# Causal attention with exact maxima: one order for maxima and exponentials, two rings of PSUM banks, and a diagonal masked in SBUF

## The reference

```
x = L0_attn_x
xn = _layernorm(x)
s = _L0_attn_ref(xn, ...)             # 16 heads of 8 features
g = _silu(_L0_ffn_ref(xn, ...))       # soft mixture of 8 experts
x = x + s * g
xn = _layernorm(x)
s = _L1_attn_ref(xn, ...)
g = _silu(_L1_ffn_ref(xn, ...))       # routed experts, a top 2 and a top half per expert
x = x + s * g

# attention, in both layers
q, k = _rope(q), _rope(k)
scores = jnp.einsum('bhqd,bhkd->bhqk', q, k) * D ** (-0.5)
scores = jnp.where(causal, scores, -jnp.inf)
weights = jax.nn.softmax(scores, axis=-1)
out = jnp.einsum('bhqk,bhkd->bhqd', weights, v)
```

## Time and profile before

| | us |
|---|---|
| three timed runs | 1244.29, 1248.29, 1241.22 (median 1244.29) |
| span of the profiled execution | 1235.5 |
| what lies around the span (median less span) | 8.8 |
| PE busy | 895.0 (72%) |
| DVE busy | 600.8 (49%) |
| ACT busy | 426.9 (35%) |
| POOL busy | 77.7 (6%) |
| attention, layer 0, first maxima to last output | about 208 to 611 |
| attention, layer 1 | about 816 to 1222 |

### The profile page before, as it was taken

One profiled execution on the slowest core, in us unless ns is written; L12 is line 12 of the kernel. 1 busy time (PEld: TensorE's weight loads), 2 busy tenths in 40 slices (PEclk: granted clock), 3 DMA queues, 4 the chain that ended last, 5 costly groups with the idle time before them and its releaser, 6 DMA issues.

```text
span 1235.5 us, 16046 instructions
## 1 busy us (share of the span) xinstructions
PE 895.0 (72%) x5604; PEld 448.6 (36%) x5604; DVE 600.8 (49%) x1338; ACT 426.9 (35%) x546; POOL 77.7 (6%) x51
## 2 busy tenths in 40 slices
PE   4377788797876967868865522947886968879786
PEld 3134576243333333433433222612333433333333
DVE  4573202663553734735172545495643725537442
ACT  1243332144424344435612400013434334344354
POOL 1710002000000000000007200000000000000000
PEclk9679998577978789889976755855978869689899
DMA  6110001001001010010022200000000010010001
GB/s 248 66 37 1 1 1 45 33 1 40 12 29 39 0 39 20 19 39 1 4 92 77 76 26 0 1 0 1 6 35 35 6 39 12 27 39 0 39 1 34
DMA packets 19563, 37.62 MB, mean 30 GB/s; under 512 B 2880, under 2 KB 12864, under 8 KB 19008
## 3 DMA queue, kind: packets, MB, share of 16 engines
q1 hardware_dynamic: 19264, 36.79, 8.2%
q10 hardware_dynamic: 256, 0.26, 0.1%
HBM read 29.44 MB, written 7.34 MB: 30 GB/s over the span
## 4 chain that ended last, share of the span: by engine, by line
PE 46%; DVE 16%; issue 16%; DMA 8%; POOL 5%; ACT 4%; SPq 4%; DVEq 0%; ACTq 0%; POOLq 0%
PE ps L939 42%; DVE maxes L882 8%; DMA R<-k_thirds 7%; SPq L435 3%; PE ps L1181 2%; SPq L437 2%; POOL rope L485 2%; POOL rope L488 1%; ACT R L633 1%; POOL third L492 1%; ACT R L628 1%; PE ps L1158 1%; DVE bnst L668 1%; ACT third L553 1%; ACT third L555 1%
## 5 line engine op out<-in xcount | busy, mean ns | idle before, releaser
L939 PE MATMUL ps<-R 128*128 128x128 f32 (+10 forms) x2240 | 568.5, 364 | 166.0 <-DMA R<-k_thirds 74.8
L882 DVE TENSOR_REDUCE maxes<-ps 128x1 f32<-128x512 f32 (+3 forms) x640 | 385.6, 635 | 321.9 <-PE ps L939 310.7
L628 ACT ACTIVATE R<-ps 128x1024 f32<-128x1024 f32 (+1 forms) x320 | 292.6, 937 | 409.8 <-PE ps L939 405.2
L939 PEld LDWEIGHTS ps<-R 74*128 74x128 bf16 (+4 forms) x2240 | 237.2, 133 | 468.6 <-issue 171.7
L939 PE MATMUL ps<-R,vgrp 128*32 128x512 f32 (+3 forms) x1536 | 176.9, 532 | 0.0
L939 PE MATMUL ps<-maskq,identb 128*128 128x128 bf16 x512 | 122.6, 257 | 0.0
L939 PE MATMUL ps<-maskk,identb 128*128 128x128 bf16 x512 | 121.8, 238 | 0.0
L939 PEld LDWEIGHTS ps<-maskk,identb 128*128 128x128 bf16 x512 | 55.0, 107 | 26.1 <-issue 16.4
L939 PEld LDWEIGHTS ps<-maskq,identb 128*128 128x128 bf16 x512 | 58.6, 114 | 5.2 <-issue 4.4
L939 PE MATMUL ps<-count,R 128*128 128x1 f32 x64 | 18.3, 357 | 54.7 <-DVE R L823 52.1
L510 POOL COPY vgrp<-vals 128x288 f32 (+1 forms) x16 | 7.1, 453 | 793.1 <-PE ps L939 793.0
(11 more groups left out here) (147 smaller groups left out, 539.0 us busy)
## 6 DMA issues: line engine op xcount, KB each, us to landing
R<-q_thirds SPq DMA_DIRECT2D x96, 96.0 KB
R<-k_thirds SPq DMA_DIRECT2D x96, 96.0 KB
R<-in_w SPq DMA_DIRECT2D x2, 2048.0 KB, 11.6
q_thirds<-third SPq DMA_DIRECT2D x8, 384.0 KB, 2.6
k_thirds<-third SPq DMA_DIRECT2D x8, 384.0 KB, 3.3
rot<-in_rot SPq DMA_DIRECT2D x1, 1024.0 KB, 5.2
R<-in_spread SPq DMA_DIRECT2D x1, 1024.0 KB, 5.7
out<-x SPq DMA_DIRECT2D x4, 256.0 KB, 2.3
```

The source lines that it names most:

```text
L628: act.activation(probs[SLOT[step]][:, h, 0:w], flat[:, 1024 * (n % 2):1024 * (n % 2) + w], ACT.Exp, scale=SCALE).then_inc(s.exp, 1)
L882: dve.tensor_reduce(dst, src, AX.X, ALU.max).then_inc(s.max_read, 1)
L939: return pe.matmul(out_, lhsT, rhs, start=first, stop=last)
```

## The change

Attention is written anew on all engines; both layers' groups are unrolled (no loop). The work of maxima, exponentials and value products stays the same in columns. In parts:

- **Maxima.** They have operands of their own, `qmx` and `kmx`, in the space of the `rope` buffers: four products (two thirds times two) of eight features, MR = 32 partitions for each head, so four heads fill the 128 partitions. A unit has two heads in a pair of banks: 1024 columns, 18 units for a group. Matmuls of the two heads alternate. Two PSUM pairs (banks 0 and 1, 2 and 3) form a ring. In the four units of diagonal blocks one matmul per bank writes the mask first and the scores are added.
- **Exponentials.** 36 units of 512 columns in a ring of three banks (4 to 6), which the shift transpose and the output transposes share. They carry no mask; GpSimd zeroes the masked triangle of `probs` with `affine_select`, ten instructions for a group. `probs` is a ring of 18 units.
- **Values.** Ten steps; queries of the first half, then of the second, both in bank 7, which ACT must have copied out between them (`pvout`).
- **Output.** ACT copies the transposed sums to `raw`; DVE divides once for each batch entry.
- **Order.** `attention_order` lays out all eight groups by estimated times.
- **Loads.** For each group 16 DMAs of 32 KB (`load_for_max`) and six of 192 KB (`load_for_exp`), each two groups ahead of their use. The two shift DMAs are issued by SyncE now, in the same list.

```diff
+UNITS, STEP = [], []
+for half in range(2):
...
+PATTERN = [[(i, 0, 512)] for i in (4, 5, 6, 7)] + [
+    [(2, 0, 256), (3, 0, 256)], [(6, 512, 256), (7, 512, 256)],
+    [(1, 0, 128), (3, 256, 128), (5, 512, 128), (7, 768, 128)],
+    [(i, P * i, 128) for i in range(4)], [(i, P * i, 128) for i in range(4, 8)]]
+NM = 2 * len(PATTERN)
...
+MAX_US, EXP_US, TOP_US, SHIFT_LAG_US, LEAD_US = 1.25, 0.56, 0.7, 3.0, 3.5
+PV_LAG, OUT_LAG = 5, 3
...
+            def load_for_max(L, g):
+                r = g % 2
+                for h in range(HG):
+                    head = slice(g * HG * D + h, (g + 1) * HG * D, HG)
+                    rows_h = slice(MR * h, MR * h + MR)
+                    for n in range(2):
+                        rows_n = slice(MR * h + 16 * n, MR * h + 16 * n + 16)
+                        sp.dma_start(qmx[rows_n, r, :],
+                                     q_dram[L][n:n + 1, head, :].to_broadcast([2, D, T])).then_inc(s_mload[r], 16)
+                        sp.dma_start(kmx[rows_n, r, :], k_dram[L][0:2, head, :]).then_inc(s_mload[r], 16)
+
+            def load_for_exp(L, g):
...
+                for i in range(3):
+                    rows_i = slice(3 * D * i, 3 * D * i + 3 * D)
+                    sp.dma_start(qop[rows_i, r, :, :].rearrange("p h t -> p (h t)"),
+                                 q_rows[i:i + 1].to_broadcast([3, D, HG * T])).then_inc(s_xload[r], 16)
+                    sp.dma_start(kop[rows_i, r, :, :].rearrange("p h t -> p (h t)"), k_rows).then_inc(s_xload[r], 16)
+
+            def attention(L):
+                cells = L * CELLS
+                for what, g, *arg in ORDER:
+                    n = L * NG + g
+                    if what == "shift":
+                        cells += 1
+                        sp.wait_ge(s_cells_read, cells)
+                        for part in range(2):
+                            sp.dma_start(qop[KR + part:KR + part + 1, g % 2, :, :],
+                                         shiftT[HG * TB * part:HG * TB * part + HG * TB, :]
+                                         ).then_inc(s_shift_in[g % 2], 16)
+                    elif what == "exp" or what == "out":
+                        cells += 1
+                        if arg[0] == NU - 1 and g + 2 < NG:
+                            sp.wait_ge(s_cells_full, cells)
+                            load_for_exp(L, g + 2)
+                    elif what == "max" and arg[0] == NM - 1 and g + 2 < NG:
+                        sp.wait_ge(s_rows_full, (n + 1) * NM)
+                        load_for_max(L, g + 2)
...
+                        if arg[0] == first + count - 1 and diagonal:
+                            slot = first % RING
+                            pool.wait_ge(s_cells_read, cells)
+                            for column in diagonal:
+                                where = probs[:, slot:slot + count, column:column + P]
+                                pool.affine_select(where, where, [[0, count], [1, P]], ALU.is_ge, 0.0, base=0,
+                                                   channel_multiplier=-1).then_inc(s_masked, 1)
...
+                    if what == "max":
...
+                        if arg[0] == 0:
+                            pe.wait_ge(s_mload[r], (L * NG // 2 + g // 2 + 1) * 16 * 16)
+                        if units >= 2:
+                            pe.wait_ge(s_rows_read, units - 1)
+                        pair = 2 * (units % 2)
+                        if diagonal:
+                            for k in range(2):
+                                mm(bank(pair + k).rearrange("p (n c) -> p n c", n=4), identb[:, :], maskq[:, :].unsqueeze(1).to_broadcast([P, 4, P]), True, False)
+                        c = 0
+                        for i, k0, w in pieces:
+                            for k, h in enumerate(heads):
+                                rows_h = slice(MR * h, MR * h + MR)
+                                last = mm(bank(pair + k)[:, c:c + w], qmx[rows_h, r, P * i:P * i + P],
+                                          kmx[rows_h, r, k0:k0 + w], not diagonal, not diagonal or c + w == BANK)
+                            c += w
+                        last.then_inc(s_rows_full, 1)
+                        units += 1
+                    elif what == "exp":
+                        if arg[0] == 0:
+                            pe.wait_ge(s_xload[r], (L * NG // 2 + g // 2 + 1) * 6 * 16)
+                            pe.wait_ge(s_shift_in[r], (L * NG // 2 + g // 2 + 1) * 2 * 16)
+                        if cells >= 3:
+                            pe.wait_ge(s_cells_read, cells - 2)
+                        for j, h, q, w, c in UNITS[arg[0]]:
+                            last = mm(bank(at)[:, c:c + w], kop[0:KM, r, h, P * j:P * j + P], qop[0:KM, r, h, q:q + w])
+                        last.then_inc(s_cells_full, 1)
+                        cells += 1
```

## The result

| | us |
|---|---|
| before, runs beside it | 1242.76 median of 4 (1239.36 to 1248.29) |
| after | 1371.63 median of 4 (1362.52 to 1373.17) |
| ratio | 1.104 (1.098 to 1.110) |
| profiled execution | span 1371.1, whole time 1373.17 |

The change makes the kernel 10% slower; 1296 was predicted, and 1371.6 lies above the range's end of 1360. The 8.8 us that the prediction put around the span are 2.1 in the execution that was profiled. In all that follows, an execution more than 1.5% above the fastest of its kernel is left out (one of e2's four, 1048.7 us, three of e4's four, 1298.4 to 1305.9, one of e7's four, 3585.6, and two of four each of e9 and e14, 1088.3 to 1110.6), and a kernel's time is the median of the rest.

A forecast was written before the change was run, and what follows sets the result against it. Bound: shift rows behind SyncE's 22 loads, steady groups 56.2 us. Changes 29.5 - 3.8 + 25.6 + 0.7 = 52 make the span 1287.5; with 8.8 around it 1296 us, range 1255 to 1335, with rivals 1180 to 1360.

The forecast's parts named there:

- the cold stretch: TensorE from a group's first exponential to its last maxima unit: 23.2 us warm, half clock adds 3.8, giving 27.0.
- its signs: In the profile: first exponentials wait 15 to 20 us for shift rows, clock 0.5 after; spacing 54 to 58 in groups 1 to 4.
- The shift behind the loads: SyncE's queue: shift rows land 29.2 us after the last maxima unit, from 11.8 issue, 16.5 data and 0.9.
- Rival (1): SyncE's queue: the shift waits for issue but not data, 9.8 us less at six boundaries per layer, 1178; chance 0.18.
- Rival (3): Loads for the maxima: the 32 KB loads crawl on one engine, 19.6 us, +73 in all, 1369; chance 0.09.
- TensorE's warm work: TensorE per group at full clock: pieces sum to 30.0 us (24.6 to 32.6), plus 1.2 of waits.
- rival (2): TensorE: strips overlap everywhere without switch cost, 4.0 us less over the 27.0, 1240, no change; chance 0.10.
- The sum: Attention per layer, from first group to last group and tail: 394.9 us together, against 365.4 and 369.3 before.
- GpSimd's mask: GpSimd zeroing masked exponentials: 3.5 to 9.4 us a group on an idle queue, hidden except in the tail.
- DVE's pitch: DVE's reductions for maxima: 1.17 us a unit, 18 units 21.1, with the final maxima 22, beside TensorE's 31.
- ACT's 22 us: ACT per group: 36 exponentials 20 us, with four small copies and the shift 22, beside TensorE's 31.
- Rival (4): Whole kernel: the plan works, no stall at first exponentials, groups of 31.2 us, time near 990; chance 0.02.

The follow-up runs named there:

- e2: Kernel after, with SyncE issuing the shift rows first and the loads of both kinds behind them: 1034.4 us, ratio 0.828.
- e4: Kernel after, with 90 unread mask matmuls (62 in the last but one group) while TensorE waits for the shift rows: 1271.0 us.
- e7: e2 plus unread mask matmuls behind the maxima units ahead of the first exponential and at the starts of groups 0 to 6: 1030.9 us, ratio 0.835.
- e9: e2 with the maxima's matmuls on 64 rows instead of 32, zeros in the other head's rows: 1077.2 us.
- e14: e2 with the maxima's matmuls on 64 rows, all data (sums over two heads, output not the reference's): 1079.6 us.
- e5: Kernel after, with the maxima's matmuls on all 128 rows (sums over four heads, output not the reference's): 1269.6 us, ratio 1.024.
- e0s: Not a run: the first exponential units of successive groups; the distance from one to the next is called a group.
- e0: Not a run: a group's first exponential unit, which waits for the shift rows.
- e3: Kernel after, with the six exponential loads moving an eighth of their columns from group 2 on (output not the reference's): 1216.5 us, ratio 0.977.
- e8: e7 plus 12 unread mask matmuls ahead of the last group's first exponential and one behind every third exponential there: 1024.3 us, ratio 0.826.
- e12: e2 with the maxima's matmuls on all 128 rows, zeros in the other heads' 96: 992.3 us, ratio 0.802.
- e6: Kernel after, with the two heads of a maxima unit one after the other instead of alternating: 1371.4 us, ratio 1.107.

## Why the prediction was wrong

**The step that failed** is the cold stretch: "half clock after a stall of 20 us adds 3.8 as in the earlier trace rows: 27.0". The runs show 10.6 instead (32.3 cold against 21.7 warm). Two things are in it. The 8.3 us of the earlier trace rows belong to a list without strips: e5, which takes the strips away, is at full clock again after 3.7 to 6.8 us and falls by 102 us, where the kernel after takes 18.8 to 34.1. And they were read from one group; five others of the same trace had shown 13.5 to 16.2 us and one 19.9, so even that list didn't support one short figure. The prediction took a time of recovery from one group of one mix of instructions and put it under another mix. Of its signs the wait came (20.3 us where 15 to 20 was said) and the spacing of e0s didn't (60.9 to 65.0 us where 54 to 58 was said). Why strips hold the clock down is open.

**The shift behind the loads: right, and nearly to the digit.** Unit 17 to e0 was to take 29.2 us; it takes 29.05 (517.86 to 546.91). Its parts were off in ways that cancel: loads come every 0.64 us and not 0.74 (16 take 10.4, not 11.8), and data and landing take the rest. That this is the cause is shown twice: by e2 (-337 us by order alone) and by the split in e3. Rival (1) is half seen: 13 of the 16 engines of a shift DMA are others than the loads' and let it pass (26 of 32 increments by 535.41), but e0 needs all 16, and the other three hold it for 13.3 us. (The prediction's sentence on those engines calls this rival the second; it is the first.) Rival (3) is refuted by the loads' own increments: the last of the 32 KB loads has landed at 531.37, 3.2 us after its issue ended. That its 1369 is nearly the time measured is luck; none of its 73 us is there.

**TensorE's warm work: a little cheaper, as rival (2) said.** 21.7 instead of 23.2: the 128-column pieces overlap, and a switch pair is 0.20. 1.5 less there and 6.8 more for the clock are the 5.3 by which e0 to unit 17 was missed. (At full clock the prediction's pieces don't agree with each other: 23.2 and 9.4 are 32.6, its sum is 31.2. Measured are 21.7 and, from unit 17 to e0's turn, 8.7; e2's warm groups take 30.8.) That each change of form has a price (0.10) agrees with the rule of the Trainium skill (TensorEngine Tiling, Key Properties) that a change of tiling mode drains TensorE. The Trainium skill (TensorE: Matmul & The Clock Gate, Why this matters for your kernels) advises to give small contractions a row group each, so that they run concurrently. The concurrency is there (0.22 for 0.44); in a list that alternates with other shapes the measured sum speaks against it, 0.42 against 0.44 before the clock is counted, and 1034 against 992 us with it.

**The sum, layer 0, predicted and measured:** first group 53.4 and 60.7; groups 1 to 4 224.8 and 249.5; group 5 49.9 and 55.7; group 6 36.4 and 38.1; last group and tail 30.4 and 33.5. Of the miss of 42.6, 39.5 are in groups 0 to 6, which all have a wait ahead of e0 (7.1 us ahead of the first, 14.7 to 21.2 ahead of the others), and 3.1 in the last group and the tail. Layer 1 misses by 43.3 in the same way. Ahead of e0 it was 236.68 where 241.4 was predicted, and layer 1's start cost 3.1 where 0.7 was; around the span 2.1 where 8.8 was. 85.9 less 4.7, plus 2.4, less 6.7, is 76.9; the profiled execution (1373.2) is 77.2 over the forecast.

**GpSimd's mask** was hidden as said: 83.4 us in 160 instructions, 5.2 a group within the bounds of 3.5 to 9.4; only in the tail does the chain go through it (1.23 us in each layer), as said. DVE's pitch and ACT's 22 us were right (22.4 and 21.4 us busy in a middle group).

**Rival (4)**, the plan that works, held 0.02. As a forecast for this kernel that was right; what the prediction lacked was that it is only one list away: e2's warm groups are 30.7.

## What to carry to other kernels

A small DMA that releases the critical path goes first on its queue, ahead of every load that is issued for later use: here the order of one engine's list was worth 337 us. A recovery time of TensorE's clock is read from rows with the same mix of matmuls or not at all, and from several groups of them, since they differed by a factor of two in one trace; and a stretch with TensorE busy throughout and a clock of 0.50 is a finding of its own. Where short contractions alternate with other matmuls, fill the contraction up with zero rows and compare: with full rows the same list lost 0.4 us a warm group (31.2 for 30.8) and kept its clock. And a DMA that is spread over many engines is as late as the fullest of them: three busy engines of 16 were enough here.

## What the runs showed of the hardware

- TensorE, busy 24.20 of 24.40 us, stays at 1.2 GHz behind a stall while its maxima run on strips of 32 rows (485.60 to 510.00). With strips it can also fall to it in a pause of 0.85 us (e8, 304.5), after which it stays down for 24 us of work. Strips don't exclude the full clock: four groups of e2 on end run at 1.00 with them (310.00 to 433.10). Strips of 64 rows do as those of 32, with data or with zeros (1079.6, 1077.2); with 128 rows no group between the first and the last loses the clock, even with zeros in 96 of them (e12, 992.3).
- A change between a strip and full rows costs 0.10 us each way; strips of 32 rows of two heads overlap in both orders that were tried (e6: 0.33 us for eight matmuls of 128 columns, 1371.4 against 1371.6).
- An 8 KB DMA issued behind six of 192 KB on the same queue lands after 13.3 us, ahead of them after 1.9 to 2.2 (e2). Of its 16 parts 13 land within some 2 us, and three, the number of engines that the loads keep busy, behind the loads' last data.
